# One letter for one instruction: the hand-written order of five engines, in place of one letter for one step

## The reference

```python
x = x + 0.5 * _L0_ffn_ref(_layernorm(x, axis=-1), ...)     # 8 experts, top 2, and a shared one
x = x + _L0_attn_ref(_layernorm(x, axis=-1), ...)          # linear attention, group norm, projection
x = x + 0.5 * _L0_ffn_ref(_layernorm(x, axis=-1), ...)
x = x + 0.5 * _L1_ffn_ref(_layernorm(x, axis=-1), ...)     # 8 experts, top 1, gelu
x = x + _L1_attn_ref(_layernorm(x, axis=-1), ...)          # RMS norm, rope, gated recurrence over 512 rows
x = x + 0.5 * _L1_ffn_ref(_layernorm(x, axis=-1), ...)
```

## Time and profile before

| | |
|---|---|
| timed, median of 3 runs | 1223.96 us (1218.2 to 1229.26) |
| profiled execution, span | 1611.3 us, 37336 instructions |
| PE, DVE, ACT, POOL busy in it | 1208.2, 1037.9, 881.7, 645.2 us |

### The profile page before, as it was taken

The page is one execution under the profiler, slowest core; times in us unless marked ns, Lnnn a source line. Parts: engine busy times, 40 slices in busy tenths (PEclk is TensorE's granted clock), DMA queues, the critical chain, the costliest instruction groups (busy, mean ns, idle before and its releaser), DMA issues.

```text
span 1611.3 us, 37336 instructions
## 1 busy us (share of the span) xinstructions
PE 1208.2 (75%) x14084; PEld 950.7 (59%) x14113; DVE 1037.9 (64%) x3441; ACT 881.7 (55%) x1505; POOL 645.2 (40%) x679
## 2 busy tenths in 40 slices
PE   3745767567766778767666766799989897989997
PEld 2423545455555666555554645677877676768776
DVE  7954655455645656666664664677767757888774
ACT  3545556334544445645543653676677445766764
POOL 1364443344555455555545453431322323342100
PEclk9876878787887978988887887898898978999989
DMA  8012323223132322222132222311210101010001
GB/s 263 14 50 62 79 68 75 59 63 83 57 84 70 78 71 76 62 65 55 57 87 67 68 67 66 76 43 46 56 46 23 28 18 33 15 29 24 2 9 34
DMA packets 172875, 93.77 MB, mean 58 GB/s; under 512 B 98516, under 2 KB 163183, under 8 KB 172575
## 3 DMA queue, kind: packets, MB, share of 16 engines
q1 hardware_dynamic: 115886, 35.64, 9.0%
q0 software_dynamic: 16384, 33.59, 7.3%
q10 hardware_dynamic: 40432, 22.17, 4.9%
HBM read 25.78 MB, written 45.61 MB: 44 GB/s over the span
## 4 chain that ended last, share of the span: by engine, by line
PE 37%; DVE 22%; ACT 13%; another core or an unknown queue 13%; issue 12%; POOL 1%; DMA 1%; ACTq 0%; POOLq 0%; DVEq 0%; SPq 0%
PE bank L759 8%; PE bank L581 3%; PE bank L820 2%; PE bank L967 2%; PE bank L806 2%; PE bank L839 2%; DVE x L1135 2%; PE bank L775 2%; PE sums L984 1%; PE sums L901 1%; PE bank L532 1%; PE sums L904 1%; ACT heads_store L1674 1%; DVE heads_store L1189 1%
## 5 line engine op out<-in xcount | busy, mean ns | idle before, releaser
L1914 POOL DMA_INDIRECT rows<-store,r_slot x256 | 258.8, 1011 | 185.1 <-DVE r_slot L1396 114.1
L759 PE MATMUL bank<-u_xp,w_hi 128*128 128x128 f16 x2432 | 267.3, 237 | 83.7 <-issue 74.0
L1930 POOL DMA_INDIRECT y_in<-ys,r_result x256 | 262.2, 1024 | 120.6 <-issue 70.3
L759 PE MATMUL bank<-u_xp,w_lo 128*128 128x128 f16 x1216 | 245.7, 237 | 34.6 <-issue 34.4
L759 PEld LDWEIGHTS bank<-u_xp,w_hi 128*128 x2432 | 212.3, 108 | 100.0 <-issue 94.4
L759 PEld LDWEIGHTS bank<-u_xp,w_lo 128*128 x1216 | 130.3, 107 | 47.1 <-issue 47.1
L581 PE MATMUL bank<-heads_store,w_hi 128*128 128x512 f16 x256 | 92.6, 449 | 7.0 <-DVE r_lg L1164 4.2
L1874 POOL TENSOR_SCALAR ve_last<-mv_last 128x4 f32<-128x4 f32 x16 | 3.1, 195 | 215.0 <-DVE mv_last L1092 214.9
L1698 ACT ACTIVATE heads_store<-bank,sc 128x512 f32<-128x512 f32 x64 | 43.3, 682 | 75.0 <-PE bank L581 41.1
L1135 DVE SCALAR_TENSOR_TENSOR x<-y_in,r_weight,x 128x128 f32<-128x128 f32 x256 | 72.5, 346 | 1.1
L1189 DVE TENSOR_TENSOR heads_store<-bank,heads_store 128x512 f32<-128x512 f32 x64 | 43.7, 686 | 42.7 <-ACT heads_store L1698 33.9
(11 more groups left out here) (434 smaller groups left out, 3478.4 us busy)
## 6 DMA issues: line engine op xcount, KB each, us to landing
ys<-u_y_even ACTq DMA_DIRECT2D x38, 256.0 KB
ys<-u_y_odd ACTq DMA_DIRECT2D x38, 256.0 KB
u_xp<-rows SPq DMA_TRANSPOSE x304
x<-x_dram SPq DMA_DIRECT2D x16, 256.0 KB, 5.6
rows<-store,r_slot POOLq DMA_INDIRECT x256
y_in<-ys,r_result POOLq DMA_INDIRECT x256
out_dram<-x SPq DMA_DIRECT2D x16, 256.0 KB
rows<-blank SPq DMA_DIRECT2D x48, 64.0 KB
```

The source lines that it names most:

```text
L759: ins = pe.matmul(B[:, of_block[j]], of_expert(wp, e, F16, part, which), xp_rows[:, xp, of_block[j]], start=(n == 0 and j == 0), stop=(n = ...
L1914: pool.indirect_dma_start(row_dram[g], bass.IndirectOffsetOnAxis(route.slot[g][:, i, t:t + 1].bitcast(U32), 0), rows[:, groups[g].first * ...
L1930: pool.indirect_dma_start(fetch.y[i][:, t, k, :], None, y_dram[g], bass.IndirectOffsetOnAxis(route.result[g][:, k, t0 + t:t0 + t + 1].bitc ...
```

## The change

Every step becomes a generator which stops (`yield`) after each instruction on DVE, ACT and POOL, and after each bank on PE, and one letter carries a lane forward to its next stop. The strings are written anew: 1293 letters for PE, 3386 for DVE, 1458 for ACT, 672 for POOL, 98 for SP. Some marks are set by tile instead of by step, so that a wait stands ahead of each instruction (`stats`, `gst`, `weighed`). SP's loads leave the lanes of units and form a lane of their own in the order of the units; `warm`, a matmul that PE did once, goes.

```diff
-                 "z": repeat(("warm", ())),
...
+        steps["z"] = [("loads", use + (k,)) for use in unit_uses for k in range(2)]
...
-        def order(engine):
-            ahead = {which: iter(steps[which]) for which in steps}
-            return [next(ahead[which]) for which in turns[engine]]
+        def played(engine, visits):
+            lanes = {which: chain.from_iterable(visits[name](*what) for name, what in steps[which] if name in visits)
+                     for which in steps}
+            for which in turns[engine]:
+                next(lanes[which])
+            assert all(next(lane, steps) is steps for lane in lanes.values())
...
                 for t in range(T):
-                    ins = dve.bn_stats(part[:, t, :], xc(c)[:, t, :])
-                mark(ins, "stats", *point)
-                on.wait_ge(*at("stats", *point))
+                    mark(dve.bn_stats(part[:, t, :], xc(c)[:, t, :]), "stats", *point, t)
+                    yield
                 for t in range(T):
+                    on.wait_ge(*at("stats", *point, t))
                     ins = dve.bn_aggr(mv[:, t, :], part[:, t, :])
-                mark(ins, "mv", *point)
+                    if t == T - 1:
+                        mark(ins, "mv", *point)
+                    yield
...
                 for i in range(2):
-                    if i:
-                        on.wait_ge(*s.by_vector.at("weighed", l, c, 0))
                     for t in range(T):
+                        if i:
+                            on.wait_ge(*s.by_vector.at("weighed", l, c, 0, t))
                         xt = x[:, c * T + t, :]
-                        ins = dve.scalar_tensor_tensor(xt, y[:, t, i, :], w[:, i, t0 + t:t0 + t + 1], xt,
-                                                       ALU.mult, ALU.add)
-                    s.by_vector.mark(ins, "weighed", l, c, i)
+                        s.by_vector.mark(dve.scalar_tensor_tensor(xt, y[:, t, i, :], w[:, i, t0 + t:t0 + t + 1], xt,
+                                                                  ALU.mult, ALU.add), "weighed", l, c, i, t)
+                        yield
...
-            def experts(l, g, u, k):
+            def loads(l, g, u, k):
                 if k == 0:
                     if u == 0:
                         clear_ends(l, g)
+                        yield
                         for i in range(3):
                             load_rows((l, g, i))
+                            yield
                 elif k == 1 and u + 3 < groups[g].units:
                     load_rows((l, g, u + 3))
+                    yield
```

More of the change, by code:

```diff
@@ L2 @@
 from contextlib import ExitStack
-from itertools import repeat
+from itertools import chain
 import numpy as np
@@ L411, in build @@
[L411 to L415, removed]
@@ L988, in values @@
                 s.by_tensor.mark(ins, "values", c, quad)
[L990 to L999 removed]
+                yield
             visits = {"prep": prepared, "head": head, "route": routed, "units": experts, "ffn1": ffn1, "front": attn1_front,
[L1002 to L1005 removed]
+                      "back": attn1_back}
+            played("tensor", visits)
         def vector_program(dve):
@@ L1076, in stats @@
             def stats(s, c, which):
-                moments(s, c, s.stats, s.mv, s.ve[:] if s in heads else None, which, c)
+                yield from moments(s, c, s.stats, s.mv, s.ve[:] if s in heads else None, which, c)
             def early(c):
@@ L1144, in head @@
                         on.wait_ge(*at("attn0", c))
-                        stats(s, c, ("ffn0", l))
+                        yield from stats(s, c, ("ffn0", l))
                 elif j == 1:
@@ L1465, in experts @@
                 if k == 1:
-                    unit_opened(use, 0, gated)
+                    yield from unit_opened(use, 0, gated)
                 elif k == 2:
-                    unit_opened(use, 1, linear)
+                    yield from unit_opened(use, 1, linear)
                 elif k == 3:
@@ L1492, in ffn1 @@
                     else:
-                        on.wait_ge(*at("weighed", 1, c, 1))
-                    stats(s, c, "ffn1")
+                        on.wait_ge(*at("weighed", 1, c, 1, T - 1))
+                    yield from stats(s, c, "ffn1")
                 elif k == 2:
@@ L1741, in experts @@
                 if k == 1:
-                    unit_widened(use, 0, s.gated)
+                    yield from unit_widened(use, 0, s.gated)
                 elif k == 2:
-                    unit_widened(use, 1, s.linear)
+                    yield from unit_widened(use, 1, s.linear)
                 elif k == 3:
@@ L2003, in sync_program @@
                              ).then_inc(cleared[g], 16)
-            visits = {"units": experts, "ffn1": ffn1}
-            for name, what in order("sync"):
-                if name in visits:
-                    visits[name](*what)
+            visits = {"loads": loads, "ffn1": ffn1}
+            played("sync", visits)
         for program in (tensor_program, vector_program, scalar_program, pool_program, sync_program):
```

482 lines of the change are left out of this document (345 added, 137 removed).

## The result

The changed kernel takes 1258.69 us in the median (1256.69 to 1259.43, four runs), the kernel before 1222.0 (1218.2 to 1229.26, four runs with the three from above): a ratio of 1.0291, 95% interval 1.025 to 1.0332. It is slower by 2.9%, where 3.3% less was forecast. All runs were made in sets with the kernel before beside them, which takes 1220 to 1224 us at a granted clock of about 0.97 in some sets and 1586 or 1620 us at about 0.85 in two others, so a ratio is read within its set.

The account below looks back on a forecast made before the run. Waits between engines, or PE's pace in some stages, were taken to bound the kernel. Terms of -15 and -27 us made -42 from 1223.96, about 1182, forecast 1184 with small parts open (-3.3%); range 1140 to 1234.

Parts of the forecast that it names:

- the 387 us: Whole kernel: profiled execution 1611.3 us against 1224 timed; nearly all the difference taken as the profiled execution's own late releases.
- Both shares that I set apart: Chain's "issue" (12%) and "another core or an unknown queue" (13%), together 403 us, taken as absent from timed runs.
- the room of the first stage: Layer 0 with its routed units, to about 1050 us: PE 30 to 80% busy, so a better order could gain.
- Term A: DVE's routing chains: 455 fewer instructions waiting for their direct forerunner, 0.115 us each, 52 us of DVE time; -15 us.
- Term B: PE's turnarounds through ACT or DVE: 54 fewer short ones, 0.5 us each (half of 0.97); -27 us.
- Term C: SP's loads, put strictly in order of units: 0, as loads run ahead of use; 5.5 us possible, left to the range.
- The second: Slower rival: 18 more tight PE turnarounds in layer 1's heads at 2.7 us each, 48 us; 1257 us, chance 0.17.
- The first rival: No change: stalls come up elsewhere and in-order queues hold up other lanes; 1212 to 1236 us, chance 0.21.
- The third: Clock rival: closing PE's gaps lifts its granted clock, 33 us off PE's chain share; 1151 us, chance 0.14.

Follow-up runs that it names:

- the gathered DVE: Changed kernel with DVE's string alone edited so each step's instructions stand together again; 1336.94 us, 1.0918 of the kernel before.
- the two runs of SP: Changed kernel with SP's loads and stores in the old order, 1266.76 us, 1.0343; all old orders with SP's in the new one, 1211.33 us, 0.9934.
- The control: All old orders in the changed code, with 28 PE banks moved one to three places at chance places, none near its source; 1230.4 us, 1.0063 of before.
- the loosened order: Changed kernel with PE's string alone edited: 40 banks moved so another bank stands in direct turnarounds; 1304.26 us, 1.0645 of before.

## Why the prediction was wrong, by its steps

**Where the time stands, and by what profile.** "I take it that nearly all of them belong to the profiled execution", of the 387 us, was half right: the execution profiled again took 1213.4 us. But it was not the profiler either, for in two sets the timed runs of the kernel before themselves take 1586 and 1620 us, and all that stood beside them is as long. What makes a set long stays open: chip 15 had a set at 1620 us and a later one at 1222, so the chip alone does not settle it. One such run, by core and by chain:

```profile
core 0: 1671.8 us, clock 0.852
```

```profile
PE 46%; DVE 17%; ACT 13%; issue 12%; another core or an unknown queue 10%; POOL 1%; DMA 1%; ACTq 0%; POOLq 0%; DVEq 0%; SPq 0%
```

Both shares that I set apart are there (12% and 10%). The shares of an undisturbed execution are other ones: DVE 38%, PE 25%, ACT 15% in the chain of before, not 22, 37 and 13. And the idle time that I took from the earlier trace rows as the room of the first stage was not in the timed runs: PE is busy 89 of 100 us from 200 to 300 there.

**Term A, -15 us.** The mechanism works and was too large. DVE's busy time is 1020.8 us with the old orders and 998.2 with the new, 22.6 less, 0.05 for each of the 455 where I had 0.115 and 52 us. That it is the interleaving which saves it is shown by the gathered DVE, where it is back at 1025. The rows that answer to the earlier trace rows, DVE in the changed kernel:

```profile
519.68 0.21 DVE L1460 TENSOR_REDUCE r_sm<-r_ex 128x8 f32<-128x64 f32 x1
519.81 0.34 DVE L1179 SCALAR_TENSOR_TENSOR x<-y_in,r_weight,x 128x128 f32<-128x128 f32 x1
...
520.42 0.20 DVE L1463 RECIPROCAL r_rc<-r_sm 128x8 f32<-128x8 f32 x1
```

The product at 519.81 starts 0.08 before the end of r_sm, as the earlier trace rows said; but r_rc, which needs r_sm, comes 0.74 us after it began and not 0.26. An interleaved chain saves DVE's time and ends later. None of the 22.6 us can be seen in the time: DVE waits 83 us more in all (229 against 146).

**Term B, -27 us, is the step that failed,** with its sign. "Together 130 and 76, 54 fewer" was miscounted: I had counted for the old order, too, the waits for free banks that the changed kernel's ring gives, which in another order of banks fall on other places. Counted for each order by itself, by inputs alone, it is 47 before (17 and 30) and 76 after (45 and 31), 29 more. The price, 0.97 us, was right: 29.1 us in 28 direct waits behind ACT. With the right count the term would have been +14 to +28, and the sum -1 to +13, where +37 was measured: counted right, the sum is a third of that at the most, and of the 45 us that the order costs the direct waits behind ACT hold 18.6. Of its sign a part came: PE's waits at the four lines that it named (L570, L772, L797, L532; now L582, L801, L827, L541) did fall, from 28.2 with the old orders to 24.1 us, while all of PE's waits rose by 45.

**Term C, 0**: right, by the two runs of SP. The new code with its waits by tile is not 0 but a gain of 0.8%, by the old orders in it; of the waits I had said only that they would not lose.

**The rivals.** The second, slower with 1257, met the time, and that is luck: its sign, the waits of L556, L591 and L626's counterparts above 66.9 us in 25 times, did not come; they are 13.5 + 5.6 + 3.1 = 22.2 us in 23 times, for 16.3 with the old orders. Its count was right in kind and its places are in the trace: direct turnarounds behind ACT went from 11 to 28 with 18.6 us more, but the price is 1.0 us and not 2.7, heads and layer 1 alike, and it is less than half of 45. The control leaves the rest of it open: moves that make no turnaround cost nearly the same, with waits elsewhere. The first rival's reason, that in-order queues hold up one another and a stall comes up elsewhere, fits the loosened order, where the time came back at other lines; its own time, no change, did not come. The third did not come: the granted clock is 0.97 in the kernel before and in the one after.

What stays open is why the new orders as a set fit less well than the old. The runs show that it is the order and not the code, that PE's waits behind ACT carry it in the trace (+39 us of +45, and 18.6 of the 39 at direct turnarounds), that both halves have it, and that no single change to one engine's string that was tried takes it back; old strings on one engine alone with new ones on the others would stop in a circle of waits and weren't tried.

The best kernels of the study are the old orders in the new code, 0.991 to 0.993 of before, with either order of loads.

## What to carry to other kernels

Five orders that were written for one another are best taken as one object: 28 chance moves by one to three places on one engine cost 1.3%, so an experiment on one string needs a control that moves as much and means nothing, with its waits compared and not only its time, and a regrained order should be kept only if it beats the old order in the new grain. Count turnarounds for each order with its own buffers; and read a profile's busy shares only after its span has been set against the timed runs, since a span that is a third longer can belong to an execution unlike the timed ones. A chain interleaved with other work saves the engine's time but ends later, which pays only if nobody waits for its end.

## What the runs showed of the hardware

The kernel before takes 1216 to 1235 us in four sets of runs and 1572 to 1640 in two others, with a granted clock of about 0.97 and 0.85. The nine traces of long executions have 9 to 14% of the chain each in "issue" and in "another core or an unknown queue"; the others have 6 to 10% and nothing. An independent DVE operation starts 0.08 us before the end of the one ahead, but 455 fewer dependent neighbours gave back 0.05 us each. The Trainium skill ("Perfetto Trace Analysis", section "Optimizing Scalar/DVE Operations") has about 60 ns of a DVE operation on SBUF overlapping the next; it does not speak of dependent neighbours. If what they lose is this overlap, the gain would be 27 us, an estimate from that page; 22.6 were measured, so it is nearer than the 52 us from the single row.
